# VectorE and ScalarE take the two halves of a step in turn, and TensorE puts the down matmuls between them

## The chip, the cores and the metric

The kernel runs on one core of a Trainium2 chip. The metric is the device time of one launch in microseconds (us). Before the change three runs took 914.65, 913.26 and 915.80 us, median 914.65.

## The reference, cut to what matters

The program is a small hybrid network on x of shape (4, 512, 128), float32. It has four layers, each with a layernorm before it and a residual after it: a state-space layer, a mixture of experts (MoE), an attention layer with 16 heads, and the same mixture of experts once more. The change touches only the two MoE layers, which compute

```
logits = xt @ router_w.T                 # xt: 2048 tokens x 128
topk_vals, topk_idx = top_k(logits, 2)
g = sigmoid(topk_vals); g = g / (g.sum(-1, keepdims=True) + 1e-10)
for e in range(8):
    ge = sum(where(topk_idx == e, g, 0), -1)
    h = silu(xt @ w_gate[e]) * (xt @ w_up[e])      # 256 wide
    out = out + ge[:, None] * (h @ w_down[e])
```

## The kernel before, in words

Every expert is computed for all tokens and weighted with its gate, which is zero where the token did not choose it. Work is laid out by channel: a step s is one expert (s // 4) and one block of 512 tokens (s % 4), so a MoE layer has 32 steps. The hidden width of 256 is two halves m = 0, 1 of 128 rows. Both matmul operands are split into a high part, rounded to fp32r, and the rest, so each product is three matmuls of 128x512.

A step runs through five queues. Each queue issues in the order in which it is written, and semaphores tie them together:

- TensorE, `moe_tensor`: `gate_up` writes, for each half, a gate bank and an up bank (L222 to L224, 12 matmuls), then `down` does the 6 matmuls (L410) of step s - 2 into the token block's own bank, which adds up over the experts. `gate_up` of half m waits for the product of half m of the step before, since that empties the banks; at an expert's first block it also waits for `w`, the split weights of the expert.
- ScalarE, `moe_scalar`: silu of each gate bank (L464), then the rounding of both halves of the gated hidden values to `hid_hi` (L471).
- VectorE, `moe_vector`: `products`, silu times up bank (L521), for both halves; then `gated`, times the expert's gate values (L527), for both halves. The gate values stand in `gate_all`, one copy for each parity of the expert, filled by a broadcast DMA.
- GpSimd, `moe_pool`: `hid_lo = hid - hid_hi` (L654), for both halves. Ahead of these two, at three blocks of four, it splits one of three pieces (256 columns) of the next expert's weights into `w_hi` (L629, times one) and `w_lo` (L632, the rest). The third piece raises `w`.
- SyncE, `moe_sync`: loads the raw weights and the gate values of the expert after next.

Steps 0 to 3 are written out by hand, interleaved with routing and with the layernorm of the last token block; steps 4 to 7 and 24 to 31 are unrolled, those between run in a loop. After step 31 the sums of the four token blocks are copied by ScalarE (`sums`, L475), transposed by TensorE (`sums_turn`, L417) and added to x by VectorE (L566). In the first MoE layer the layernorm of block 0 follows at once, and attention starts from it.

Of the kernel before, what the change touches and what calls it, by code (L numbers as in the profile page):

```python
# [15 lines left out]
ACT = mybir.ActivationFunctionType  # L16
ALU = mybir.AluOpType

P = 128
BANK = 512  # L20
# [13 lines left out]
def build(nc, t, out):  # L34
# [17 lines left out]
    with ExitStack() as ctx:  # L52
# [328 lines left out]
        def moe_tensor(pe, k, meanwhile):  # L381


            q, ln = MOE[k], 2 * k + 1

            def gate_up(i, j, first):
# [4 lines left out]
                for m in range(MT):  # L391
# [36 lines left out]
            gate_up(0, 1, True)  # L428
            ln_turn(pe, ln, 3)
            gate_up(0, 2, True)  # L430
            route_logits(pe, k, 3)
            route_turn(pe, k, 3)
            down(0, 2, True)
            down(0, 3, True)
            route_gates(pe, k, 3)
            gate_up(0, 3, True)
            for j in range(4, 8):
                gate_up(0, j, True)
                down(0, j, True)
            with pe.Fori(1, HALF - 1) as i:  # L440
                for j in range(8):
                    gate_up(i, j, False)
                    down(i, j, False)
            for j in range(8):
                gate_up(HALF - 1, j, False)
                down(HALF - 1, j, False)

            sums_turn(0)
            down(HALF, 0, False)
            sums_turn(1)  # L450
            down(HALF, 1, False)
            sums_turn(2)
            sums_turn(3)

        def moe_scalar(act, k):

            q, ln = MOE[k], 2 * k + 1

            def silus(s, first):
                for m in range(MT):  # L460
                    act.wait_ge(q["g"], 2 * s + m + 1)
                    if not first:
                        act.wait_ge(q["mul"], 2 * s - 1 + m)
                    nc.scalar.activation(silu[:, m, :], bank[2 * m][:, :], ACT.Silu).then_inc(q["sg"], 1)  # L464

            def highs(s, buf, first):
                for m in range(MT):
                    act.wait_ge(q["gm"], 2 * s + m + 1)
                    if not first:
                        act.wait_ge(q["d"], s - 1)  # L470
                    nc.scalar.copy(hid_hi[:, buf, m, :], hid[:, buf, m, :]).then_inc(q["hi"], 1)  # L471

            def sums(c):
                act.wait_ge(q["d"], (E - 1) * CH + c + 1)
# [16 lines left out]
            gates_copy(act, k, 3)  # L491
            highs(2, 0, False)
            silus(3, False)
            highs(3, 1, False)
            for j in range(4, 8):
                silus(j, False)
                highs(j, j % 2, False)
            with act.Fori(1, HALF - 1) as i:
                for j in range(8):
                    silus(8 * i + j, False)  # L500
                    highs(8 * i + j, j % 2, False)
            for j in range(8):
                s = 8 * (HALF - 1) + j
                silus(s, False)
                if j == 7:
                    sums(0)
                highs(s, j % 2, False)
            for c in range(1, CH):
                sums(c)

        def moe_vector(dve, k, last_rows):

            q, ln = MOE[k], 2 * k + 1

            def products(s, buf, first):
                for m in range(MT):
                    dve.wait_ge(q["sg"], 2 * s + m + 1)
                    dve.wait_ge(q["u"], 2 * s + m + 1)
                    if not first:
                        dve.wait_ge(q["hl"], 2 * s - 3 + m)  # L520
                    nc.vector.tensor_tensor(hid[:, buf, m, :], silu[:, m, :], bank[2 * m + 1][:, :],  # L521
                                            ALU.mult).then_inc(q["mul"], 1)

            def gated(s, buf, par, c):
                for m in range(MT):
                    dve.wait_ge(q["mul"], 2 * s + m + 1)
                    nc.vector.tensor_tensor(hid[:, buf, m, :], hid[:, buf, m, :],  # L527
                                            gate_all[:, par, c * BANK:(c + 1) * BANK], ALU.mult).then_inc(q["gm"], 1)
# [27 lines left out]
            first_gates(3)  # L556
            gated(3, 1, 0, 3)
            for j in range(4, 8):
                products(j, j % 2, False)
                gated(j, j % 2, j // CH, j % CH)  # L560
            with dve.Fori(1, HALF) as i:
                body(i)
            for c in range(CH):
# [55 lines left out]
        def moe_pool(pool, k):  # L619
# [1 line left out]

            PIECES = [(0, FH), (FH, 2 * FH), (2 * FH, EW)]

            def split(e_count, ld_value, par, piece, waits):

                lo, hi = PIECES[piece]
                waits()
                pool.wait_ge(q["ld0"] if par == 0 else q["ld1"], ld_value)
# [8 lines left out]
            def body(i, first, last):  # L637
                for j in range(8):
                    s, par, c, buf = 8 * i + j, j // CH, j % CH, j % 2
                    if c < 3 and not (last and par == 1):  # L640

                        def waits():
                            if first and par == 0:
                                return
                            if c < 2:
                                pool.wait_ge(q["u"], 8 * (2 * i + par))
                            else:
                                pool.wait_ge(q["d"], 4 * (2 * i + par))
                        split(2 * i + par + 1, 48 * i + 48 * (1 + par), 1 - par, c, waits)
                    for m in range(MT):  # L650
# [3 lines left out]
                        nc.gpsimd.tensor_tensor(hid_lo[:, buf, m, :], hid[:, buf, m, :],  # L654
                                                hid_hi[:, buf, m, :].bitcast(F32), ALU.subtract).then_inc(q["hl"], 1)

            for piece in range(3):
                split(0, 48, 0, piece, lambda: None)
# [709 lines left out]
```

## Time and profile before

| what | value |
|---|---|
| time of the profiled execution | 913.67 us |
| its span, first to last instruction | 911.9 us |
| median of the three runs | 914.65 us |
| mean granted TensorE clock | 0.966 of full speed |
| TensorE busy, whole span | 823.7 us, 90% |
| VectorE | 646.0 us, 71% |
| ScalarE | 497.5 us, 55% |
| GpSimd | 449.7 us, 49% |
| first MoE layer | about 76 to 243 us of the span |
| second MoE layer | about 745 to 911.9 us |

The busy figures are over the whole span, attention included. What the change is worth is read from the two MoE stretches alone: which engine or wait sets the length of a step there. A TensorE matmul that follows another shows about 0.39 us each but starts 0.23 us after it, so start-to-start times are the ones to use. A group "x2" gives the time of two instructions together.

### The profile page before, as it was taken

The numbers are of one execution on the slowest core, as the hardware profiler recorded it, in microseconds if no ns is written. First come the engines' busy times: TensorE is split into PE (matmuls) and PEld (weight loads), VectorE is DVE, ScalarE is ACT, GpSimd is POOL, SyncE is SP. The second block draws the span as 40 slices with busy tenths as digits, with TensorE's granted clock in tenths as the row PEclk, the third lists the DMA queues.
The fourth block names the chain that finished last, engine by engine and source line by source line (L and its number), as shares of the span: only waits on it lengthen the run. The fifth ranks groups of instructions, "written<-read, shape, count | busy, mean of one in ns | idle before, by whom it ended". The sixth has DMA issues, their size and how long they took to land.

```text
span 911.9 us, 13922 instructions
## 1 busy us (share of the span) xinstructions
PE 823.7 (90%) x4320; PEld 544.0 (60%) x4320; DVE 646.0 (71%) x1664; ACT 497.5 (55%) x1079; POOL 449.7 (49%) x506
## 2 busy tenths in 40 slices
PE   1867689999889999999999999999999995899997
PEld 0555477777655556556556565565555554677776
DVE  7998477767788776767876767767777655667775
ACT  2214354455467766666666665666656634454554
POOL 2350489988334333333333333334333324799984
PEclk9688899999999999999999999999999998999999
DMA  7000335546400000000000000000000012546321
GB/s 208 3 1 28 86 73 81 86 79 205 165 1 1 1 2 1 1 1 1 1 1 1 1 2 1 1 1 1 1 1 1 2 42 72 98 77 79 79 66 46
DMA packets 53265, 36.40 MB, mean 40 GB/s; under 512 B 2209, under 2 KB 50721, under 8 KB 53201
## 3 DMA queue, kind: packets, MB, share of 16 engines
q1 hardware_dynamic: 53200, 35.61, 17.1%
q8 instruction: 33, 0.54, 0.2%
q14 instruction: 32, 0.25, 0.1%
HBM read 34.35 MB, written 1.25 MB: 39 GB/s over the span
## 4 chain that ended last, share of the span: by engine, by line
PE 58%; DVE 13%; issue 12%; POOL 10%; DMA 3%; ACT 2%; POOLq 1%; SPq 0%; ACTq 0%; DVEq 0%
PE bank L805 13%; PE bank L788 11%; PE bank L775 11%; POOL hid_lo L654 7%; PE bank L222 6%; PE bank L224 4%; PE bank L223 4%; PE bank L741 3%; POOL w_hi L629 3%; PE bank L410 2%; DMA gates<-gatesT 1%; DVE x_norm L263 1%; DVE hid L527 1%; DVE hid L521 1%; DMA gate_all<-gates 1%
## 5 line engine op out<-in xcount | busy, mean ns | idle before, releaser
L994 POOL TENSOR_SCALAR prob<-prob,inv_total 128x512 f32<-128x512 f32 x256 | 174.3, 694 | 316.7 <-DVE inv_total L839 316.7
L943 ACT ACTIVATE prob<-prob,peak 128x512 f32<-128x512 f32 x256 | 185.9, 726 | 46.9 <-DVE peak L850 46.9
L654 POOL TENSOR_TENSOR hid_lo<-hid,hid_hi 128x512 fp32r<-128x512 f32 x128 | 163.1, 1294 | 90.5 <-ACT hid_hi L471 90.2
L850 DVE CUSTOM_DVE_ANT_0 prob<-bank,bias_band 128x512 f32<-128x512 f32 x256 | 166.6, 688 | 31.3 <-PE bank L775 25.2
L471 ACT CAST hid_hi<-hid 128x512 fp32r<-128x512 f32 x128 | 78.8, 621 | 140.7 <-DVE hid L527 138.5
L521 DVE TENSOR_TENSOR hid<-silu,bank 128x512 f32<-128x512 f32 x128 | 82.8, 684 | 81.8 <-ACT silu L464 73.8
L805 PE MATMUL bank<-probT,v 128*64 128x512 f32 x512 | 139.2, 624 | 0.8 <-ACT oT L954 0.8
L788 PE MATMUL bank<-ident,prob 128*128 128x128 f32 x1024 | 135.5, 276 | 3.0 <-ACT probT L949 1.8
L788 PEld LDWEIGHTS bank<-ident,prob 128*128 128x128 f32 x1024 | 118.6, 141 | 23.5 <-issue 6.7
L527 DVE TENSOR_TENSOR hid<-hid,gate_all 128x512 f32<-128x512 f32 x128 | 115.9, 944 | 15.8 <-DMA gate_all<-gates 15.8
L222 PE MATMUL bank<-xT_hi,w_hi 128*128 128x512 f32 x256 | 106.8, 417 | 14.1 <-DVE hid L521 14.1
L224 PE MATMUL bank<-xT_hi,w_lo 128*128 128x512 f32 x256 | 103.1, 403 | 0.0
L223 PE MATMUL bank<-xT_lo,w_hi 128*128 128x512 f32 x256 | 102.8, 402 | 0.0
L857 DVE COPY probT<-bank 128x512 f32<-128x512 f32 x128 | 87.6, 684 | 20.7 <-PE bank L788 20.7
L775 PEld LDWEIGHTS bank<-qkT_hi 64*128 64x128 f32 x256 | 24.0, 184 | 101.7 <-issue 93.4
L938 ACT CAST qkT_hi<-bank 128x512 fp32r<-128x512 f32 x64 | 37.7, 589 | 80.0 <-PE bank L224 79.9
L949 ACT COPY probT<-bank 128x512 f32<-128x512 f32 x128 | 73.4, 574 | 14.4 <-PE bank L788 14.4
L464 ACT ACTIVATE silu<-bank 128x512 f32<-128x512 f32 x128 | 69.9, 592 | 6.6 <-PE bank L224 6.3
L222 PEld LDWEIGHTS bank<-xT_hi,w_hi 128*128 128x128 f32 x256 | 49.0, 191 | 38.7 <-DVE hid L521 22.7
L839 DVE RECIPROCAL inv_total<-total 128x2 f32<-128x2 f32 x128 | 21.2, 166 | 65.9 <-ACT prob L943 65.1
L775 PE MATMUL bank<-qkT_hi 64*128 64x512 f32 x256 | 64.4, 500 | 0.0
L224 PEld LDWEIGHTS bank<-xT_hi,w_lo 128*128 128x128 f32 x256 | 49.3, 192 | 11.6
(170 smaller groups left out, 1284.3 us busy)
## 6 DMA issues: line engine op xcount, KB each, us to landing
gate_all<-gates SPq DMA_DIRECT2D x12, 1024.0 KB, 15.6
bias_band<-bias_rows SPq DMA_DIRECT2D x16, 448.0 KB, 11.5
gate_all<-gates SPq DMA_DIRECT2D x16, 256.0 KB, 4.9
w_raw<-in_w_gate SPq DMA_DIRECT2D x16, 128.0 KB, 14.4
w_raw<-in_w_up SPq DMA_DIRECT2D x16, 128.0 KB, 10.7
w_raw<-in_w_down SPq DMA_DIRECT2D x16, 128.0 KB, 8.6
x_res<-in_x SPq DMA_DIRECT2D x4, 256.0 KB, 4.9
out<-x_res SPq DMA_DIRECT2D x4, 256.0 KB, 2.3
```

The costliest lines, as they stand in the source:

```text
L222: nc.tensor.matmul(dst, lh, rh, start=start, stop=False)
L223: nc.tensor.matmul(dst, lh, rl, start=False, stop=False)
L224: return nc.tensor.matmul(dst, ll, rh, start=False, stop=stop)
L521: nc.vector.tensor_tensor(hid[:, buf, m, :], silu[:, m, :], bank[2 * m + 1][:, :], ALU.mult).then_inc(q["mul"], 1)
L527: nc.vector.tensor_tensor(hid[:, buf, m, :], hid[:, buf, m, :], gate_all[:, par, c * BANK:(c + 1) * BANK], ALU.mult).then_inc(q["gm"], 1)
L654: nc.gpsimd.tensor_tensor(hid_lo[:, buf, m, :], hid[:, buf, m, :], hid_hi[:, buf, m, :].bitcast(F32), ALU.subtract).then_inc(q["hl"], 1)
L775: last = nc.tensor.matmul(bank[2 * (n % 2) + h][:, :], ql[rows, u % 2, 0, q], kl[rows, u % 2, 1, :], start=(i == 0), stop=(i == 2))
L788: last = nc.tensor.transpose(bank[4 + h][:, j * P:(j + 1) * P], prob[:, n % PROBS, h, j * P:(j + 1) * P], ident[:, :])
L805: last = nc.tensor.matmul(bank[PV_BANK][h * DK:(h + 1) * DK, :], v[:, kt, col], probT[:, u % 2, h, kt, :], start=(kt == 0), stop=(kt == QT ...
L850: nc.vector.tensor_tensor_reduce(out=prob[:, buf, h, :], in0=bank[2 * (n % 2) + h][:, :], in1=row_bias, scale=-1.0, scalar=NEG_START, op0= ...
L943: nc.scalar.activation(prob[:, buf, h, :], prob[:, buf, h, :], ACT.Exp, bias=peak[:, buf, h:h + 1], scale=-1.0, accum_out=total[:, buf, h: ...
L994: nc.gpsimd.tensor_scalar(prob[:, buf, h, :], prob[:, buf, h, :], inv[:, buf, h:h + 1], 1.0, ALU.mult, ALU.mult).then_inc(a_n, 1)
```

## The change

Four things are done to the same computation.

1. TensorE: a step is now gate and up of half 0, then `down` of step s - 2, then gate and up of half 1 (steps 4 to 31).
2. VectorE: product of half 0, gating of half 0, product of half 1, gating of half 1 (steps 4 to 31). At an expert's first block the wait for the gate values moves ahead of the first product.
3. ScalarE: silu of half 0, rounding of half 1 of the step before, silu of half 1, rounding of half 0. After step 31 the copy of the first sum stands ahead of the last rounding.
4. GpSimd: the split of a weight piece moves from ahead of both subtractions to between them, while its waits stay ahead of the first. `w_hi` is made by a tensor_scalar (times the per-partition one, times 1.0) where it was a tensor_tensor with the one broadcast.

```diff
+            def step(i, j, first):
+                gate_up(i, j, first, [0])
+                down(i, j, first)
+                gate_up(i, j, first, [1])
...
             with pe.Fori(1, HALF - 1) as i:
                 for j in range(8):
-                    gate_up(i, j, False)
-                    down(i, j, False)
+                    step(i, j, False)
...
+            def step(s, j):
+                silu_of(s, 0, False)
+                high(s - 1, (j - 1) % 2, 1, False)
+                silu_of(s, 1, False)
+                high(s, j % 2, 0, False)
...
-                silus(s, False)
-                if j == 7:
-                    sums(0)
-                highs(s, j % 2, False)
+                step(8 * (HALF - 1) + j, j)
+            sums(0)
+            high(8 * HALF - 1, 1, 1, False)
...
+            def step(s, j):
+                for m in range(MT):
+                    product(s, j % 2, m, False)
+                    gate(s, j % 2, m, j // CH, j % CH)
...
                 for j in range(8):
-                    products(8 * i + j, j % 2, False)
                     if j % CH == 0:
                         dve.wait_ge(q["bc0"] if j < CH else q["bc1"], 16 * i)
-                    gated(8 * i + j, j % 2, j // CH, j % CH)
+                    step(8 * i + j, j)
...
-                nc.gpsimd.tensor_tensor(w_hi[:, par, lo:hi], w_raw[:, par, lo:hi], ones[:, :].to_broadcast([P, hi - lo]),
+                nc.gpsimd.tensor_scalar(w_hi[:, par, lo:hi], w_raw[:, par, lo:hi], ones[:, :], 1.0, ALU.mult,
                                         ALU.mult).then_inc(q["sp"], 1)
...
+                    splits = c < 3 and not (last and par == 1)
+                    for m in range(MT):
+                        if m == 0 and splits:
+
+                            pool.wait_ge(q["ld1"] if par == 0 else q["ld0"], 48 * i + 48 * (1 + par))
...
                         nc.gpsimd.tensor_tensor(hid_lo[:, buf, m, :], hid[:, buf, m, :],
                                                 hid_hi[:, buf, m, :].bitcast(F32), ALU.subtract).then_inc(q["hl"], 1)
-
+                        if m == 0 and splits:
+                            split(2 * i + par + 1, 1 - par, c)
```

## Rows read from the trace of the kernel before

**Rows 1.** Windows view, one expert: window, length, busy time of PE, PEld, DVE, ACT, POOL.
```profile
163.00:181.00 18.00, 17.52 (x74) 13.34 (x73) 12.90 (x18) 8.91 (x17) 16.48 (x15) 1.00 0.46 85
```

**Rows 2.** Waits, 120 to 232 us: us in total, times, longest.
```profile
ACT hid_hi L471 <- DVE hid L527: 55.1, 42, 2.5
```

**Rows 3.** Chain that ended last, 140 to 180 us: start us, us, what.
```profile
158.33 1.11 DVE hid L527
...
159.99 0.60 ACT silu L464
...
160.70 0.70 DVE hid L521
...
161.44 0.50 PE bank L222
```

**Rows 4.** Timeline of PE in step 15, starts of steps 16 and 20: start us, us.
```profile
161.78 0.39 PE L223 MATMUL bank<-xT_lo,w_hi 128*128 128x512 f32 x1
162.01 0.39 PE L224 MATMUL bank<-xT_hi,w_lo 128*128 128x512 f32 x1
...
166.12 0.50 PE L222 MATMUL bank<-xT_hi,w_hi 128*128 128x512 f32 x1 [0.25 <-DVE hid L521]
...
183.99 0.50 PE L222 MATMUL bank<-xT_hi,w_hi 128*128 128x512 f32 x1 [0.24 <-DVE hid L521]
```

**Rows 5.** Timeline of DVE, gatings beside a weight split and a shorter pair.
```profile
161.90 2.20 DVE L527 TENSOR_TENSOR hid<-hid,gate_all 128x512 f32<-128x512 f32 x2
...
170.84 1.78 DVE L527 TENSOR_TENSOR hid<-hid,gate_all 128x512 f32<-128x512 f32 x2
```

**Rows 6.** Timeline of POOL, the same stretch.
```profile
159.99 2.54 POOL L654 TENSOR_TENSOR hid_lo<-hid,hid_hi 128x512 fp32r<-128x512 f32 x2
162.50 1.06 POOL L629 TENSOR_TENSOR w_hi<-w_raw,ones 128x256 fp32r<-128x256 f32 x1
163.63 1.07 POOL L632 TENSOR_TENSOR w_lo<-w_raw,w_hi 128x256 fp32r<-128x256 f32 x1
```

**Rows 7.** Timeline, ACT and then POOL: a rounding and the subtraction it releases.
```profile
225.22 1.22 ACT L471 CAST hid_hi<-hid 128x512 fp32r<-128x512 f32 x2 [1.63 <-DVE hid L527]
225.91 2.55 POOL L654 TENSOR_TENSOR hid_lo<-hid,hid_hi 128x512 fp32r<-128x512 f32 x2 [1.28 <-ACT hid_hi L471]
```

**Rows 8.** Groups by shape on POOL: count, busy us, mean ns.
```profile
L994 POOL TENSOR_SCALAR prob<-prob,inv_total 128x512 f32<-128x512 f32 x256 | 174.3, 694 | 316.7 <-DVE inv_total L839 316.7
...
L1168 POOL TENSOR_TENSOR bT_hi<-bT,ones 128x256 fp32r<-128x256 f32 x1 | 0.6, 612 | 0.1
...
L1168 POOL TENSOR_TENSOR router_hi<-ssm_par,ones 128x8 fp32r<-128x8 f32 x1 | 0.2, 197 | 0.0
```

**Rows 9.** Timeline: gatings of step 3 (DVE), start of step 5 (PE).
```profile
113.44 1.29 DVE L527 TENSOR_TENSOR hid<-hid,gate_all 128x512 f32<-128x512 f32 x2 [4.25 <-DMA gate_all<-gates]
116.66 0.50 PE L222 MATMUL bank<-xT_hi,w_hi 128*128 128x512 f32 x1 [3.50 <-DVE hid L521]
```

**Rows 10.** Timeline of step 31, first MoE: PE, PE, ACT, DVE, DVE.
```profile
232.42 0.40 PE L222 MATMUL bank<-xT_hi,w_hi 128*128 128x512 f32 x1
...
240.16 0.50 PE L410 MATMUL bank<-hid_hi,w_hi 128*128 128x512 f32 x1 [0.85 <-POOL hid_lo L654]
...
234.00 1.32 ACT L464 ACTIVATE silu<-bank 128x512 f32<-128x512 f32 x2
...
235.57 0.69 DVE L521 TENSOR_TENSOR hid<-silu,bank 128x512 f32<-128x512 f32 x1 [0.17 <-PE bank L224]
...
237.38 0.69 DVE L566 TENSOR_TENSOR x_res<-bank,x_res 128x512 f32<-128x512 f32 x1
```

**Rows 11.** Timeline of PE, starts of steps 5 and 31, second MoE.
```profile
782.06 0.50 PE L222 MATMUL bank<-xT_hi,w_hi 128*128 128x512 f32 x1 [3.10 <-DVE hid L521]
...
897.67 0.40 PE L222 MATMUL bank<-xT_hi,w_hi 128*128 128x512 f32 x1
```

**Rows 12.** DMA issues: count, KB each, median us to landing.
```profile
gate_all<-gates SPq DMA_DIRECT2D x12, 1024.0 KB, 15.6
```

More of the change, by code:

```diff
@@ L384, in moe_tensor, with gate_up @@
             q, ln = MOE[k], 2 * k + 1
-            def gate_up(i, j, first):
+            def gate_up(i, j, first, halves=range(MT)):
                 s, par, c = 8 * i + j, j // CH, j % CH
@@ L390, in gate_up @@
                     pe.wait_ge(q["w"], 2 * i + par + 1)
-                for m in range(MT):
+                for m in halves:
                     if not (first and j == 0):
@@ L436, in moe_tensor @@
             gate_up(0, 3, True)
+            def step(i, j, first):
+                gate_up(i, j, first, [0])
+                down(i, j, first)
+                gate_up(i, j, first, [1])
             for j in range(4, 8):
-                gate_up(0, j, True)
-                down(0, j, True)
+                step(0, j, True)
             with pe.Fori(1, HALF - 1) as i:
                 for j in range(8):
-                    gate_up(i, j, False)
-                    down(i, j, False)
+                    step(i, j, False)
             for j in range(8):
-                gate_up(HALF - 1, j, False)
-                down(HALF - 1, j, False)
+                step(HALF - 1, j, False)
             sums_turn(0)
@@ L457, in moe_scalar, with silu_of, high @@
             q, ln = MOE[k], 2 * k + 1
+            def silu_of(s, m, first):
+                act.wait_ge(q["g"], 2 * s + m + 1)
+                if not first:
+                    act.wait_ge(q["mul"], 2 * s - 1 + m)
+                nc.scalar.activation(silu[:, m, :], bank[2 * m][:, :], ACT.Silu).then_inc(q["sg"], 1)
             def silus(s, first):
                 for m in range(MT):
[L461 to L464, printed above, removed]
+                    silu_of(s, m, first)
+            def high(s, buf, m, first):
+                act.wait_ge(q["gm"], 2 * s + m + 1)
+                if not first:
+                    act.wait_ge(q["d"], s - 1)
+                nc.scalar.copy(hid_hi[:, buf, m, :], hid[:, buf, m, :]).then_inc(q["hi"], 1)
             def highs(s, buf, first):
                 for m in range(MT):
[L468 to L471, printed above, removed]
+                    high(s, buf, m, first)
+            def step(s, j):
[3 more added lines that the diff above has]
+                high(s, j % 2, 0, False)
             def sums(c):
@@ L513, in moe_vector, with product, gate @@
             q, ln = MOE[k], 2 * k + 1
+            def product(s, buf, m, first):
+                dve.wait_ge(q["sg"], 2 * s + m + 1)
+                dve.wait_ge(q["u"], 2 * s + m + 1)
+                if not first:
+                    dve.wait_ge(q["hl"], 2 * s - 3 + m)
+                nc.vector.tensor_tensor(hid[:, buf, m, :], silu[:, m, :], bank[2 * m + 1][:, :],
+                                        ALU.mult).then_inc(q["mul"], 1)
             def products(s, buf, first):
                 for m in range(MT):
[L517 to L522, printed above, removed]
+                    product(s, buf, m, first)
+            def gate(s, buf, m, par, c):
+                dve.wait_ge(q["mul"], 2 * s + m + 1)
+                nc.vector.tensor_tensor(hid[:, buf, m, :], hid[:, buf, m, :],
+                                        gate_all[:, par, c * BANK:(c + 1) * BANK], ALU.mult).then_inc(q["gm"], 1)
             def gated(s, buf, par, c):
                 for m in range(MT):
-                    dve.wait_ge(q["mul"], 2 * s + m + 1)
-                    nc.vector.tensor_tensor(hid[:, buf, m, :], hid[:, buf, m, :],
-                                            gate_all[:, par, c * BANK:(c + 1) * BANK], ALU.mult).then_inc(q["gm"], 1)
+                    gate(s, buf, m, par, c)
+            def step(s, j):
+                for m in range(MT):
+                    product(s, j % 2, m, False)
+                    gate(s, j % 2, m, j // CH, j % CH)
             def body(i):
                 for j in range(8):
-                    products(8 * i + j, j % 2, False)
                     if j % CH == 0:
                         dve.wait_ge(q["bc0"] if j < CH else q["bc1"], 16 * i)
-                    gated(8 * i + j, j % 2, j // CH, j % CH)
+                    step(8 * i + j, j)
             def first_gates(c):
@@ L558, in moe_vector @@
             for j in range(4, 8):
-                products(j, j % 2, False)
-                gated(j, j % 2, j // CH, j % CH)
+                step(j, j)
             with dve.Fori(1, HALF) as i:
@@ L622, in moe_pool, with split @@
             PIECES = [(0, FH), (FH, 2 * FH), (2 * FH, EW)]
-            def split(e_count, ld_value, par, piece, waits):
+            def split(e_count, par, piece):
                 lo, hi = PIECES[piece]
-                waits()
-                pool.wait_ge(q["ld0"] if par == 0 else q["ld1"], ld_value)
-                nc.gpsimd.tensor_tensor(w_hi[:, par, lo:hi], w_raw[:, par, lo:hi], ones[:, :].to_broadcast([P, hi - lo]),
+                nc.gpsimd.tensor_scalar(w_hi[:, par, lo:hi], w_raw[:, par, lo:hi], ones[:, :], 1.0, ALU.mult,
                                         ALU.mult).then_inc(q["sp"], 1)
@@ L639, in body @@
                     s, par, c, buf = 8 * i + j, j // CH, j % CH, j % 2
[L640 to L645, printed above, removed]
+                    splits = c < 3 and not (last and par == 1)
+                    for m in range(MT):
+                        if m == 0 and splits:
+                            pool.wait_ge(q["ld1"] if par == 0 else q["ld0"], 48 * i + 48 * (1 + par))
+                            if not (first and par == 0) and c < 2:
                                 pool.wait_ge(q["u"], 8 * (2 * i + par))
-                            else:
+                            elif not (first and par == 0):
                                 pool.wait_ge(q["d"], 4 * (2 * i + par))
-                        split(2 * i + par + 1, 48 * i + 48 * (1 + par), 1 - par, c, waits)
-                    for m in range(MT):
                         pool.wait_ge(q["hi"], 2 * s + m + 1)
@@ L655, in body @@
                                                 hid_hi[:, buf, m, :].bitcast(F32), ALU.subtract).then_inc(q["hl"], 1)
+                        if m == 0 and splits:
+                            split(2 * i + par + 1, 1 - par, c)
+            pool.wait_ge(q["ld0"], 48)
             for piece in range(3):
-                split(0, 48, 0, piece, lambda: None)
+                split(0, 0, piece)
             body(0, True, False)
```

8 lines of the change are left out of this document (2 added, 6 removed).

## The prediction

> **What bounds the kernel now.** I read the page first for where the change lies: two MoE layers, about 167 us each. The windows view of one expert [rows 1] shows TensorE busy 17.5 of 18 us, GpSimd 16.5, VectorE only 12.9. That looks like a full TensorE, but start to start a matmul takes 0.23 us [rows 4], so the 18 matmuls of a step need 18 x 0.232 = 4.18 us, and step 15 to step 16 takes 4.68 [rows 3, 4]. Four steps take 17.87 us (166.12 to 183.99, steps 16 to 20 [rows 4]) against 16.7 of matmul issue.
>
> What fills the 0.5 us is in the waits and the chain. ScalarE waits for VectorE's gating 42 times, 55 us in all [rows 2], and TensorE at each of these starts for VectorE's product [rows 4]. The chain [rows 3] gives the loop: second gating ends 159.44, rounding, silu 159.99 (0.53 after the rounding began), product 160.70 (0.71 later), next step's first matmul 161.44 (0.74 later). VectorE then does two products (160.70 to 161.90, 1.20) and two gatings (2.20) [rows 5]. Sum: 0.02 + 0.53 + 0.71 + 1.20 + 2.20 = 4.66. So in the old order silu(s+1, 0) stands behind both roundings of step s, and all of VectorE's step is in that loop.
>
> The 2.20 hides a second limit. Gatings take 1.10 us each there, but two took 1.78 where no split went before, and 0.60 each, start to start, where GpSimd is idle (235.57 plus 0.60, two gatings, 237.38 [rows 10]). Put the rows of VectorE and GpSimd side by side [rows 5, 6]: subtractions 159.99 to 162.50; gating asked for at 161.90 moves at 162.50 and is through at 163.03; w_hi, started 162.50, ends at 163.56 though such a split takes 0.61 alone [rows 8]; the next gating ends at 164.1; w_lo at about 164.67; then the next subtraction. The two engines go strictly in turn. Holding times are 1.25 for a subtraction, 0.53 for a gating, 0.53 for w_hi, 0.57 for w_lo, and 2 x 1.25 + 2 x 0.53 + 0.53 + 0.57 + 0.02 = 4.68, which is the step. Products, which read a PSUM bank, are always 0.69 and take no part.
>
> This is where the Trainium skill speaks against the change. "SBUF — State Buffer", section "Who interferes with whom", says that GpSimd and a VectorE instruction with two SBUF inputs share one port pair as an exclusive lock, held for the whole instruction. The trace agrees: 1.06 and 1.07 for splits that take 0.61 and 0.72 alone. By a reading without that rule (gating always 0.6) the new order would leave nothing but matmul issue.
>
> **The change, part by part.** I take the loops of the new order with these times. Let gate and up of half 0 of an expert's first step start at 0.
>
> *TensorE.* Same instructions. Half 0 from 0 (0.11 longer after a stall, 0.34 against 0.23 [rows 3, 4]), down 1.5, half 1 2.9, next step 4.29. Product(s, 0) has until then, so the old wait of TensorE for products goes: product comes at about 1.9 and 4.7.
>
> *ScalarE.* silu starts 0.45 after the third matmul of its bank starts: in step 31 that matmul starts at 232.42 + 8 x 0.232 = 234.28 and the second silu at 235.32 - 0.59 = 234.73 [rows 10]. So silu(s, 1) starts at 2.89 + 0.46 + 0.45 = 3.8, and rounding(s, 0) stands behind it, at 4.3, though its gating was through at about 3.3. Subtraction(s, 0) follows 0.69 after the rounding [rows 7], at 5.0. This cost is new: TensorE now brings half 1 1.39 us later, and half 0 waits with it.
>
> *VectorE.* Same instructions. A gating now directly follows its own product, so the product's whole 0.69 plus about 0.04 counts and not 0.60: estimate 0.13 more for each half. VectorE has room: 2 x (0.73 + 0.53) plus port waits, in 4.18. I put it at nothing by itself; it is in the walk below.
>
> *GpSimd.* The tensor_scalar of 256 columns is not in the trace. 512 columns take 694 ns, and a tensor_tensor with the broadcast one takes 197 at 8 columns and 612 at 256 [rows 8]. Below: half of 694, 347 ns, with 0.08 less holding as for the old w_hi, or 0.27. Above: no saving, 0.53. On a line from 197 at 8 to 694 at 512 it is 197 + 497 x 248/504 = 442 ns; with 0.05 off, between the two offsets seen (0.08 for w_hi, 0.04 for the subtraction), I take holding 0.39. That is nearest to the row of its own kind. The Trainium skill ("GPSIMD Engine Reference", section 3.1) gives about 1.03 cycles per element at 1.2 GHz for one input. Its slope taken from the 694 would give 0.47 us alone, so 0.42 held, and 1 us more in the sum.
>
> *The weight split is moved behind subtraction(s, 0).* This is the step that decides. TensorE's first step of the next expert waits for the third piece (w_lo of block 2). Everything from subtraction of block 0 to there goes through the port, in turn with the gatings that ask meanwhile. Walk: subtraction(0, 0) 5.00 to 6.25; gating(0, 1), asked 5.37, to 6.78; w_hi to 7.17, 0.07 own wait, w_lo to 7.81; gating(1, 0) to 8.34; subtraction(0, 1) to 9.59; gating(1, 1) to 10.12; subtraction(1, 0) to 11.37; gating(2, 0) to 11.90; split to 12.93; subtraction(1, 1) to 14.18; gating(2, 1) to 14.71; subtraction(2, 0) to 15.96; gating(3, 0) to 16.49; split to 17.52. As a sum: 5.00 + 5 x 1.25 + 6 x 0.53 + 3 x (0.39 + 0.07 + 0.57) = 17.52. TensorE would be there at 16.70. In the old order the split ended at 164.67 and step 16 started at 166.12, 1.45 us to spare. So the new order trades 17.87 for 17.57 per expert: TensorE runs three steps at 4.18 to 4.29 and then stalls about 0.87 for `w`.
>
> *From step 5 to step 31.* Before: 232.42 - 116.66 = 115.76 and 897.67 - 782.06 = 115.61 [rows 9 to 11], which is 26 x 4.18 = 108.7, 1.67 of step 5 (it takes 5.85 in both layers, partly at the lower clock after TensorE's wait; unchanged) and 5.3 of stalls. The old kernel had little loss in its first and last steps; the new one stalls at each of six expert boundaries (steps 8, 12, ... 28). After: 108.7 + 1.67 + 6 x 0.87 = 115.6. Difference -0.1 per layer, where a full cure would be -5.3.
>
> *Step 5.* Gatings of step 3 end their wait for the DMA at 113.44 [rows 9], and silu(4, 0) stood behind two roundings; now behind one: -0.53 per layer.
>
> *End of a layer.* Half 1 of step 31 comes after down of step 29. Let step 31 start at 0. silu(31, 1) 3.7, product(31, 1) 4.5 (0.59 after the last up matmul starts [rows 10]), gating asked 5.26; subtraction(31, 0) asks at 5.23 and, if first, holds until 6.48. Then the gating is through at 7.0, and only then comes VectorE's first add to x, which was at 237.38 - 232.42 = 4.96. The last down starts at 9.05 (before: 240.16 - 232.42 = 7.74). If the gating is first, they are 6.15 and 8.35. The requests are 0.03 apart, so I take the middle. The layernorm of block 0 hangs on the add, and attention on it: +1.6 in the first layer. In the second the last down decides: +0.95.
>
> *DMAs.* None changes, but VectorE now waits for an expert's gate values before its first product. They are asked for when the expert before last is gated: from 6.0 of one step to 1.9 of the fifth step after, 5 x 4.36 + 1.9 - 6.0 = 17.7 us, against 15.6 to landing [rows 12]. Hidden, with 2 us to spare.
>
> *Sum.* 2 x (-0.1 - 0.53) + 1.6 + 0.95 = +1.3. On the profiled execution 913.67 that is 915.0; it lies 1.0 under the median of the runs, so I forecast 914.65 + 1.3 = 916.
>
> **Rivals.** (A) The forecast: the `w` wait takes the place of the loop over VectorE and ScalarE. Bounds of the split's holding, 0.27 to 0.53, change the three splits of six experts in two layers, 36 x 0.12 = -4.3 to 36 x 0.14 = +5.0; the middle of that and the tail's 0.8 either way give 912 to 920.
> (B) TensorE becomes the bound: the split is in time because gatings find the port free (fewer than six in the chain; two fewer are enough with a cheaper w_hi). For it: 16.5 of 18 us of GpSimd shrinks by 3 x 0.14 per expert, and the old split had 1.45 us to spare. Against: the walk. Full price 2 x (-5.3 - 0.53) + 2.55 = -9.1, so 905.5; half cured 910.
> (C) Slower: the tensor_scalar is no cheaper in the chain than the broadcast (holding 0.53). Its place is the chain from subtraction(0, 0) to `w`; price 36 x 0.14 = +5.0 and the tail's upper end +0.8: 922. Slower by over 0.3% from a holding of 0.39 + 1.4/36 = 0.43 on. For it: hardly anything under 0.43 is proved by a row; against: 694 ns at 512 columns.
> (D) The gate values' wait, now ahead of the product: if landing exceeds 17.7 us by one, six loads in two layers cost 12 us, 928. The median of 15.6 speaks against.
> That the change does not do what it says, the two engines staying in lockstep through the port, would give A's time too.
>
> **How the numbers follow.** A measurement of this kernel can tell about 0.3%, 2.7 us: below 911.9 and above 917.4. A 0.55 (within 0.38, slower 0.10, faster 0.07), B 0.25 (faster), C 0.17 and D 0.03 (slower). Faster 0.32, same 0.38, slower 0.30. The range 906 to 922 leaves out the fullest form of B and the far ends of C and D; A alone is 912 to 920.
>
> **What would show it.** Right: steps of 4.18 three times and one of about 4.9 at each expert's start, TensorE's idle time there put down to GpSimd's w_lo (L632 in the old file), no more waits of TensorE for products; subtraction(s, 0) starting about 5.0 after its step; w_hi about 0.44 where alone. Wrong: boundary steps of 4.18 (B), a w_hi of 0.6 (C), VectorE waiting for gate_all inside the loop (D), or a gating that overlaps a subtraction, which would break the walk's rule of turns.

## The result, and the profile after

The changed kernel takes 919.37 us (median of 18 runs, 916.22 to 922.79) against 914.75 for the kernel before: ratio 1.0049, 95% interval 1.0037 to 1.0061, so 4.6 us slower. The forecast was 916.0, 1.3 us more than before and within what counts as no change. The time lies in the forecast's range; the loss is three and a half times the one forecast, and the interval leaves no doubt that it is a loss.

The profiled execution took 920.07 us, span 918.2 (before 913.67 and 911.9). The first thing to look at is where TensorE's steps start. Timeline of PE in the changed kernel, starts of steps 16 to 20, which answer to [rows 4]:

```profile
168.05 0.49 PE L222 MATMUL bank<-xT_hi,w_hi 128*128 128x512 f32 x1 [0.44 <-POOL w_lo L649]
...
172.32 0.40 PE L222 MATMUL bank<-xT_hi,w_hi 128*128 128x512 f32 x1
...
176.49 0.39 PE L222 MATMUL bank<-xT_hi,w_hi 128*128 128x512 f32 x1
...
180.74 0.39 PE L222 MATMUL bank<-xT_hi,w_hi 128*128 128x512 f32 x1
...
182.54 0.50 PE L410 MATMUL bank<-hid_hi,w_hi 128*128 128x512 f32 x1 [0.24 <-POOL hid_lo L669]
...
186.03 0.50 PE L222 MATMUL bank<-xT_hi,w_hi 128*128 128x512 f32 x1 [0.43 <-POOL w_lo L649]
```

The steps take 4.27, 4.17, 4.25 and 5.29: three at TensorE's own pace, and one long one that ends in a wait for `w_lo`, the last piece of the next expert's weights. The long step loses time twice: `down` (the line at 182.54) starts 0.41 us late because it waits for `hid_lo` of two steps before, then the next step starts 0.60 late for `w_lo`, and a restart after a wait costs 0.11. The forecast had the whole loss as one wait for `w`. Both hang on the same queue of GpSimd and `w_lo` comes last, so the end of that queue still sets the length. An expert takes 17.98 us, where it took 17.87. The old pattern, a stall for VectorE's product at two steps of four [rows 4], is gone.

The waits of the same stretch, 120 to 235 us, answer to [rows 2]: who waited for whom, us in total, times, longest.

```profile
ACT silu L465 <- PE bank L224: 39.5, 49, 2.6
DVE hid L530 <- PE bank L224: 16.1, 19, 2.3
ACT hid_hi L475 <- DVE hid L539: 15.1, 22, 1.2
DVE hid L530 <- POOL hid_lo L669: 7.4, 6, 1.3
POOL hid_lo L669 <- ACT hid_hi L475: 5.8, 9, 1.3
PEld bank L410 <- POOL hid_lo L669: 4.8, 11, 0.7
PEld bank L222 <- issue: 3.5, 4, 0.9
PE bank L222 <- POOL w_lo L649: 2.5, 6, 0.5
PEld bank L222 <- POOL w_lo L649: 1.6, 2, 0.8
PE bank L410 <- POOL hid_lo L669: 1.2, 5, 0.2
```

ScalarE waited 55 us for gatings before and 15 now; silu and product now wait mostly for TensorE. TensorE has two new waits, both for GpSimd: the matmul that waits for `w_lo`, six times, once at each expert boundary, and `down` that waits for `hid_lo` (4.8 us of its weight loads and 1.2 of its matmuls; waits of loads overlap matmuls, so these do not add up). The change does what it says, and the wait that ends last at a boundary is the forecast's.

The chain that leads to it, GpSimd's timeline (answers to [rows 6]):

```profile
173.08 1.29 POOL L669 TENSOR_TENSOR hid_lo<-hid,hid_hi 128x512 fp32r<-128x512 f32 x1 [0.52 <-ACT hid_hi L475]
174.34 0.92 POOL L646 TENSOR_SCALAR w_hi<-w_raw,ones 128x256 fp32r<-128x256 f32 x1
175.35 0.74 POOL L649 TENSOR_TENSOR w_lo<-w_raw,w_hi 128x256 fp32r<-128x256 f32 x1
176.05 3.45 POOL L669 TENSOR_TENSOR hid_lo<-hid,hid_hi 128x512 fp32r<-128x512 f32 x2
179.48 0.92 POOL L646 TENSOR_SCALAR w_hi<-w_raw,ones 128x256 fp32r<-128x256 f32 x1
180.49 0.74 POOL L649 TENSOR_TENSOR w_lo<-w_raw,w_hi 128x256 fp32r<-128x256 f32 x1
181.19 2.99 POOL L669 TENSOR_TENSOR hid_lo<-hid,hid_hi 128x512 fp32r<-128x512 f32 x2
184.16 0.92 POOL L646 TENSOR_SCALAR w_hi<-w_raw,ones 128x256 fp32r<-128x256 f32 x1
185.17 0.73 POOL L649 TENSOR_TENSOR w_lo<-w_raw,w_hi 128x256 fp32r<-128x256 f32 x1
```

Read it against the walk of the prediction. The first subtraction of the expert starts 173.08 - 168.05 = 5.03 us after its step (5.00 forecast). From it on the chain holds five subtractions (the four behind the first are two pairs, 3.45 and 2.99 instead of 2.5 because gatings go between), three w_hi of 0.92 and three w_lo, and TensorE starts 0.13 after the last w_lo ends at 185.90. GpSimd has no idle time in between but 0.09 between each w_hi and its w_lo. The windows view of this expert, columns as in [rows 1], has GpSimd, its waits for the port included, at 17.2 of 18.0 us, more than TensorE's matmul issue of 16.7:

```profile
168.05:186.03 17.98, 17.31 (x72) 13.32 (x73) 13.94 (x17) 9.41 (x17) 17.21 (x15) 1.00 0.34 84
```

At the end of the first layer (answers to [rows 10]): step 31 starts at 234.47, and the lines are of PE, DVE, DVE.

```profile
234.47 0.39 PE L222 MATMUL bank<-xT_hi,w_hi 128*128 128x512 f32 x1
...
243.52 0.50 PE L410 MATMUL bank<-hid_hi,w_hi 128*128 128x512 f32 x1 [0.21 <-POOL hid_lo L669]
...
239.74 1.73 DVE L539 TENSOR_TENSOR hid<-hid,gate_all 128x512 f32<-128x512 f32 x1
241.38 0.68 DVE L585 TENSOR_TENSOR x_res<-bank,x_res 128x512 f32<-128x512 f32 x1
```

The last gating took 1.73 where it takes 0.69 alone: the subtraction was first at the port. The first add to x comes 6.91 us after step 31 starts (before 4.96), the last down 9.05 (before 7.74).

### The profile page after: what moved, and what is told of

It reads as the page before. It is cut to its first block, busy times and chain, and to the rows that moved or that the text cites. A ratio compares the mean times of both kernels' runs of the same rounds, so it can differ in the third digit from the quotient of the medians.

```text
span 918.2 us, 13922 instructions
## 1 busy us (share of the span) xinstructions
PE 826.7 (90%) x4320; PEld 545.8 (59%) x4320; DVE 667.8 (73%) x1664; ACT 503.2 (55%) x1079; POOL 462.9 (50%) x506
## 4 chain that ended last, share of the span: by engine, by line
PE 57%; POOL 16%; DVE 11%; issue 10%; DMA 3%; ACT 2%; POOLq 1%; SPq 0%; ACTq 0%; DVEq 0%
PE bank L823 13%; PE bank L806 11%; PE bank L793 11%; POOL hid_lo L669 11%; PE bank L222 6%; PE bank L224 4%; PE bank L223 4%; POOL w_hi L646 4%; PE bank L759 3%; PE bank L410 3%; DMA gates<-gatesT 1%; POOL w_lo L649 1%; DVE x_norm L263 1%; DMA gate_all<-gates 1%; DVE ln_stats L237 1%
## 5 line engine op out<-in xcount | busy, mean ns | idle before, releaser
L669 POOL TENSOR_TENSOR hid_lo<-hid,hid_hi 128x512 fp32r<-128x512 f32 x128 | 193.8, 1532 | 81.8 <-ACT hid_hi L475 81.8
L539 DVE TENSOR_TENSOR hid<-hid,gate_all 128x512 f32<-128x512 f32 x128 | 133.7, 1050 | 20.2 <-DMA gate_all<-gates 16.3
L530 DVE TENSOR_TENSOR hid<-silu,bank 128x512 f32<-128x512 f32 x128 | 86.9, 684 | 60.4 <-PE bank L224 32.7
L465 ACT ACTIVATE silu<-bank 128x512 f32<-128x512 f32 x128 | 76.0, 598 | 87.0 <-PE bank L224 86.9
L222 PE MATMUL bank<-xT_hi,w_hi 128*128 128x512 f32 x256 | 104.8, 409 | 13.4 <-DVE hid L530 8.4
L410 PE MATMUL bank<-hid_hi,w_hi 128*128 128x512 f32 x128 | 55.4, 433 | 3.6 <-POOL hid_lo L669 3.5
```

Of the source, the lines that this page charges most:

```text
L222: nc.tensor.matmul(dst, lh, rh, start=start, stop=False)
```

## The experiments

All kernels were timed in five rounds beside the kernel before; a ratio is to that kernel, with its 95% interval. Its median was 914.95 us beside experiments 1, 2, 3 and 5, 914.23 beside 6, 7, 8 and 10, and 915.22 beside 4, 9 and 11. Lengths of steps and experts are of one profiled execution each.

**1. The changed kernel with the old w_hi.**

```diff
-                nc.gpsimd.tensor_scalar(w_hi[:, par, lo:hi], w_raw[:, par, lo:hi], ones[:, :], 1.0, ALU.mult,
-                                        ALU.mult).then_inc(q["sp"], 1)
+                nc.gpsimd.tensor_tensor(w_hi[:, par, lo:hi], w_raw[:, par, lo:hi], ones[:, :].to_broadcast([P, hi - lo]),
+                                        ALU.mult).then_inc(q["sp"], 1)
```

> The changed kernel with w_hi made by the old tensor_tensor (times the broadcast one); all else as changed. My theory: TensorE's stall at an expert's first step is the end of a chain of subtractions, gatings and splits that take GpSimd's and VectorE's port in turn, and each w_hi in it holds 0.53 instead of 0.39 us. So three splits per expert add 0.42 us to the 17.98 of an expert, 6 boundaries in two layers 5 us: about 9.5 us over the kernel before (+1.0%), boundary steps of 5.7 us. Rival 1, the stall is made by TensorE's and ScalarE's new order alone and GpSimd only follows: no difference from the changed kernel, +4.6 us. Rival 2, the tensor_scalar itself is what costs: back to the kernel before or under it.

Measured: 923.24 us, ratio 1.0094 (1.0068 to 1.0119), 8.3 us over before. w_hi takes 1.06 again, an expert 18.35 us (starts of steps 16 and 20 at 165.59 and 183.94). Three w_hi, each 0.14 us longer, make an expert 0.37 longer, so nearly all of it goes into TensorE's wait. So the chain through the port is what TensorE waits for, and rivals 1 and 2 fall.

**2. The changed kernel with the split ahead of the first subtraction.**

```diff
-                        if m == 0 and splits:
-                            split(2 * i + par + 1, 1 - par, c)
+                    if splits:
+                        split(2 * i2 + par + 1, 1 - par, c)
```

Here i2, par and c are those of the next step; the waits of the split stand ahead of the second subtraction, and the first split of a layer is done at once.

> The changed kernel with each split piece put back ahead of its step's first subtraction (right behind the last subtraction of the step before, its waits ahead of that subtraction), tensor_scalar kept. My theory: the chain to the third piece loses one subtraction and one gating (1.72 us), and GpSimd does w_hi in the 0.5 to 1.3 us in which it waited for the first rounding. TensorE's `w` stall goes, and the port's total sets the pace, about 17.45 us per expert against 17.98: 2 to 3 us under the kernel before, 7 under the changed one. Rival 1 (the order of the other engines alone): stays at +4.6. Rival 3 (the two engines' total port time is the limit wherever the split stands): 17.9 per expert, 1 us from the changed kernel.

Measured: 911.41 us, ratio 0.9965 (0.9949 to 0.9982): 3.5 us under before, about 8 under the changed kernel. An expert takes 17.34 us (164.71 to 182.05). GpSimd's timeline of it:

```profile
169.84 0.47 POOL L646 TENSOR_SCALAR w_hi<-w_raw,ones 128x256 fp32r<-128x256 f32 x1
170.40 0.74 POOL L649 TENSOR_TENSOR w_lo<-w_raw,w_hi 128x256 fp32r<-128x256 f32 x1
171.10 3.46 POOL L670 TENSOR_TENSOR hid_lo<-hid,hid_hi 128x512 fp32r<-128x512 f32 x2
174.54 0.48 POOL L646 TENSOR_SCALAR w_hi<-w_raw,ones 128x256 fp32r<-128x256 f32 x1
175.10 1.06 POOL L649 TENSOR_TENSOR w_lo<-w_raw,w_hi 128x256 fp32r<-128x256 f32 x1
...
179.10 0.92 POOL L646 TENSOR_SCALAR w_hi<-w_raw,ones 128x256 fp32r<-128x256 f32 x1
180.10 0.74 POOL L649 TENSOR_TENSOR w_lo<-w_raw,w_hi 128x256 fp32r<-128x256 f32 x1
```

Two of the three w_hi now meet no gating (0.47 and 0.48 us instead of 0.92), and one subtraction fewer stands in the chain to the third piece. Of the parts undone in these experiments the new place of the split cost most. The remaining stall (4.70 at the first step of each expert) is for hid_lo; the wait for `w_lo` is gone. The expectation held, with a little more gain than expected; rivals 1 and 3 fall. The new orders of VectorE and of ScalarE were never undone alone, so what each is worth is open.

**3. The kernel before with only the tensor_scalar.** The split's waits stand one subtraction earlier, as in experiment 2.

> The kernel before with only w_hi changed to a tensor_scalar (the split stands where it stood, its waits one subtraction earlier). My theory: each of three splits per expert gives 0.14 us back to the port, so steps of 4.66 become 4.5: 36 x 0.13 = 4.6 us under the kernel before, 910. Rival 2 (the tensor_scalar costs): slower than before. Rival 4 (the old loop over VectorE and ScalarE, 4.66, does not hang on the port): no difference.

Measured: 917.75 us, ratio 1.0034 (1.0019 to 1.0049), slower. This expectation failed. Timelines of DVE and POOL in that kernel:

```profile
162.62 2.26 DVE L527 TENSOR_TENSOR hid<-hid,gate_all 128x512 f32<-128x512 f32 x2
...
163.72 1.44 POOL L627 TENSOR_SCALAR w_hi<-w_raw,ones 128x256 fp32r<-128x256 f32 x1
165.24 0.74 POOL L630 TENSOR_TENSOR w_lo<-w_raw,w_hi 128x256 fp32r<-128x256 f32 x1
```

Both gatings went ahead of the tensor_scalar, which ended at 165.16, 0.28 after the second one. With the tensor_tensor [rows 5, 6] one gating went ahead of w_hi and one ahead of w_lo, and w_lo's own start-up lay behind the latter. Now w_lo starts into a free port and pays it: 2.53 + 1.44 + 0.08 + 0.69 = 4.74 a step against 4.68. So the turns are not strict, though my prediction had them so. Why the tensor_scalar lets both pass was not tried.

**4. The control to 3: same placement, w_hi by the old tensor_tensor.**

> The control to the run of the kernel before with tensor_scalar, which was slower by 2.8 us where 4.6 us of gain were expected: the same placement (split behind the last subtraction of the step before, its waits one subtraction earlier), but w_hi by the old tensor_tensor. My reading now: in that run the tensor_scalar took 1.44 us beside two gatings, both of which went ahead of it, so its short holding was given back by w_lo starting cold. Then this control is equal to the kernel before within 0.2%. Rival: the moved waits cost, then this one is slower by 2 to 3 us too.

Measured: 915.84 us, ratio 1.0011 (0.9998 to 1.0023). DVE and POOL in this kernel, at the same place as in 3:

```profile
162.32 2.20 DVE L527 TENSOR_TENSOR hid<-hid,gate_all 128x512 f32<-128x512 f32 x2
...
162.90 1.08 POOL L627 TENSOR_TENSOR w_hi<-w_raw,ones 128x256 fp32r<-128x256 f32 x1
164.06 1.07 POOL L630 TENSOR_TENSOR w_lo<-w_raw,w_hi 128x256 fp32r<-128x256 f32 x1
```

The moved waits explain at most a small part. The intervals of 3 and 4 touch, so the times alone don't settle the rest; the profiles do: steps 16 to 20 take 18.05 us in 3, 17.83 here and 17.87 before, and both w_hi and w_lo have their old lengths here. With the placement the same, the longer steps are the tensor_scalar's.

**5. `w` raised after the second piece.**

```diff
-                if piece == 2:
+                if piece == 1:
                     last.then_inc(q["w"], 1)
+                if piece == 2:
+                    last.then_inc(q["wd"], 1)
```

> The changed kernel with `w` raised after the second piece (gate and up weights), and a semaphore of its own for the third, on which the down matmuls and the next load wait. My theory: the wait of TensorE at an expert's first step goes, but GpSimd is busy 17.2 of 18 us per expert with its waits for the port, so the subtractions become late instead and TensorE waits for hid_lo: 17.8 per expert, +2 us on the kernel before, 2 to 3 us under the changed one. Rival 5 (the `w` wait is the whole loss): 16.7 per expert, 7 us under the kernel before. Rival 1 (order alone): +4.6.

Measured: 916.28 us, ratio 1.0014 (0.9999 to 1.0029), 17.80 us per expert (163.45 to 181.25), as expected. The longest wait of TensorE in it, in total:

```profile
PEld bank L412 <- POOL hid_lo L673: 8.1, 15, 0.7
```

The `w` wait is gone, and the wait of down for hid_lo, 4.8 us in the changed kernel, grew to 8.1: it now comes at two steps of an expert, the first and the last, 0.4 us each. An expert is only 0.18 us shorter. The semaphore was only where GpSimd's queue showed.

**6. ScalarE makes w_hi, in the new order.**

```diff
+            def weights_high(i, j, last):
...
+                nc.scalar.copy(w_hi[:, 1 - par, lo:hi], w_raw[:, 1 - par, lo:hi]).then_inc(q["sp"], 1)
...
                 high(s, j % 2, 0, False)
+                weights_high(i, j, last)
```

> The changed kernel, but from step 4 on ScalarE makes w_hi (a copy, after its rounding of half 0), and GpSimd only w_lo. My theory (the port's turns set the pace): each split leaves 0.9 us less on GpSimd and one turn of the port less, GpSimd's work falls under TensorE's, the `w` wait goes and an expert takes TensorE's own 16.7 us. Together 9 to 10 us under the kernel before, 905; what stays is the longer end of a layer (1.2 us in the first). Rival 1 (the order of the queues alone costs): no better than +4.6. Rival 6 (ScalarE becomes late, 9.4 of 18 us busy plus 3 x 0.37): TensorE waits for silu or product, 17.5 or more per expert.

**7. The same in the old order**, `weights_high` between silus and highs.

> The kernel before, but from step 4 on ScalarE makes w_hi between its silus and its roundings, and GpSimd only w_lo; queues otherwise in the old order. My theory: the old loop over VectorE and ScalarE (two products, two gatings, rounding, silu: 4.66) shrinks to 3.7 to 4.2 once gatings wait less for the port, so TensorE's 4.18 bounds: 10 us under the kernel before, 904, equal to the same edit in the new order or 0.6 better by its shorter end. Rival 7 (the old order is bound by its own loop whatever the port does, so the new order is needed for the gain): 4.5 per step, at most 4 us under before, and clearly over the same edit in the new order.

Measured: 905.10 us, ratio 0.9891 (0.9871 to 0.9912), and 904.80 us, ratio 0.9894 (0.9874 to 0.9913). Windows of one expert in each, new order first:

```profile
161.23:177.97 16.74, 16.74 (x73) 13.37 (x72) 12.91 (x16) 10.31 (x21) 15.38 (x12) 1.00 0.50 79
```

```profile
163.86:180.58 16.72, 16.72 (x74) 13.56 (x72) 11.62 (x17) 9.75 (x19) 13.54 (x12) 1.00 0.57 87
```

TensorE is busy all the time in both, at 4.18 a step. w_hi costs ScalarE 0.41 us, and GpSimd is at 13.5 to 15.4 us. Both orders reach the same 16.7, so the order of the queues is not what kept the kernel before from it. In the old order the pairs of gatings take 1.3 to 1.9 us instead of up to 2.2, and the loop over VectorE and ScalarE is shorter by as much. Rivals 1, 6 and 7 fall.

**8. The kernel before with only TensorE's new order.**

```diff
-                    gate_up(i, j, False)
+                    gate_up(i, j, False, [0])
                     down(i, j, False)
+                    gate_up(i, j, False, [1])
```

> The kernel before with only TensorE's queue in the new order (gate and up of half 0, down, half 1). My theory: half 1 comes 1.39 us later, its silu and product too, and both gatings and all GpSimd work of the step stand behind it; port turns and the loop then give about 18.3 us per expert: 7 to 9 us over the kernel before. Rival 2 (order on TensorE is free, the loss is in the moved split): no difference from the kernel before.

Measured: 926.84 us, ratio 1.0116 (1.0093 to 1.0140), 12.6 us slower, where 7 to 9 were expected. Steps 16 to 20 start 18.18 us apart (167.75 to 185.93), and the five experts of steps 8 to 28 take 18.28 on average, as expected. In the profiled execution the two layers' ends are 1.4 us longer each, which the expectation left out, and attention, which the edit doesn't touch, took 503.1 us against 498.8; why stays open. One turn of the loop, DVE, DVE, ACT, PE:

```profile
172.38 0.69 DVE L524 TENSOR_TENSOR hid<-silu,bank 128x512 f32<-128x512 f32 x1 [0.80 <-POOL hid_lo L657]
172.98 1.88 DVE L530 TENSOR_TENSOR hid<-hid,gate_all 128x512 f32<-128x512 f32 x2
...
174.36 1.15 ACT L474 CAST hid_hi<-hid 128x512 fp32r<-128x512 f32 x2 [2.24 <-DVE hid L530]
...
176.88 0.50 PE L222 MATMUL bank<-xT_hi,w_hi 128*128 128x512 f32 x1 [0.52 <-DVE hid L524]
```

The product of half 1 comes late, both gatings stand behind it, both roundings behind them, and the next step's silu and product behind those. A rounding that waits 2.24 us is no sign by itself: before, the longest waited 2.5 [rows 2]. What is longer is TensorE's own wait for the product, here 0.68 us late by its start, against 0.36 to 0.52 in the kernel before.

**9. The changed kernel with TensorE's old order.**

> The changed kernel with TensorE's queue back in the old order (gate and up of both halves, then down); VectorE, ScalarE and GpSimd as changed. My theory: half 1 comes 1.39 us earlier, so its silu, the rounding of half 0 behind it and the whole port chain start earlier; the `w` stall shrinks to about 0.4 us more than TensorE's own time per expert of 17.2 to 17.6 us: within 1 us of the kernel before, 4 us under the changed one. Rival (TensorE's order is what lets products come in time): slower than the changed kernel.

Measured: 916.34 us, ratio 1.0012 (0.9995 to 1.0029), 17.69 us per expert (167.17 to 184.86). The time is as expected; the expert is just above the expected 17.2 to 17.6, and the way is another than I named:

```profile
ACT hid_hi L474 <- PE bank L410: 39.2, 25, 2.4
```

The rounding of half 0 waits for down of step s - 2, which frees hid_hi and comes last in TensorE's old order. So the first subtraction starts 5.31 us after its expert's first step (172.48 - 167.17), not earlier than 5.03. What is shorter is the chain behind it, 12.38 us against 12.95, with five gatings in it instead of six. TensorE then waits only for `w_lo`. TensorE's new order costs the changed kernel about 3 us (0.3%), though it takes away the wait of the rounding for down.

**10. Short splits.** The changed kernel, splits of experts 2 to 7 cut to 8 of 256 columns.

> The changed kernel with the weight splits of experts 2 to 7 cut to the first 8 of each piece's 256 columns (the rest of the split is left out, so stale weights are used); all waits, queues and semaphores stay. It measures what the splits' port time costs. My theory: with about 0.4 us per split instead of 1.7, TensorE bounds at 4.18 a step: 8 to 9 us under the kernel before. Rival 1 (the order costs by itself, splits or not): +4.6, or at least slower than before.

Measured: 904.11 us, ratio 0.9885 (0.9863 to 0.9906), 16.7 us per expert from step 8 on, 4.18 a step. Between the first and the last steps of a layer the order costs nothing once the splits' port time is gone.

**11. The end of a layer in the old order**, in the changed kernel and in that of experiment 6: TensorE gate_up of both halves before down, VectorE products before gatings, the first sum ahead of both roundings, in step 31 only.

> The changed kernel with only the last step of each layer back in the old order. My theory: of the change's loss the two ends make 1.95 and 1.3 us; they go, the `w` stalls stay: about 1.5 us over the kernel before (+0.15%), 3 us under the changed one. Rival: the ends are hidden, then no difference from the changed kernel.

> The changed kernel with w_hi made by ScalarE from step 4 on (as in the earlier run of that edit in the new order, 905.1), and its last step of each layer in the old order: TensorE gate and up of both halves, then down; VectorE both products, both gatings; ScalarE the first sum ahead of both roundings. My theory: the end of a layer grew because the last gating waits behind a subtraction for the port; with it back (first add to x at 5.0 instead of 6.8 us after step 31 starts, last down at 7.8 instead of 9.0) 2 to 3 us come off: about 903, the fastest of all. Rival: the end of the first layer is hidden by other work, then 904.5.

Measured: 919.59 us, ratio 1.0047 (1.0029 to 1.0065), and 904.34 us, ratio 0.9884 (0.9863 to 0.9905). Against the changed kernel (1.0049) and experiment 6 (0.9891) no difference can be told. Timeline of DVE at the end of the first layer of the former, where step 31 starts at 233.06:

```profile
234.04 1.77 DVE L544 TENSOR_TENSOR hid<-hid,gate_all 128x512 f32<-128x512 f32 x1
235.72 0.68 DVE L535 TENSOR_TENSOR hid<-silu,bank 128x512 f32<-128x512 f32 x1
...
238.90 0.68 DVE L593 TENSOR_TENSOR x_res<-bank,x_res 128x512 f32<-128x512 f32 x1
```

The last gating of step 30 still waits for a subtraction (1.77) and step 31 inherits it; the add comes at 5.84 instead of 6.91, not 4.96. In the profiled executions the end gives back 0.5 us of the way to attention's first matmul (14.43 after step 31's start, 14.98 in the changed kernel, 13.56 before) and 0.45 in the second layer. My expectations of 3 us and of 2 to 3 us were wrong.

## Why the prediction was right in kind and off in size

**The bound of the kernel before.** Right, with a correction. Port turns and the VectorE-ScalarE loop give 4.68 at the two steps of four that stall; experiments 6, 7 and 10 take work off the port and reach 4.18. I had called the port a "second limit"; experiment 7 shows it was the only one that had to go: shorter gatings shorten the loop too. The lock is there as the Trainium skill ("SBUF — State Buffer", section "Who interferes with whom") has it: 1.06 us for a w_hi beside a gating and 0.61 alone. Its rule spoke for the right side. My addition that the turns are strict fell in experiment 3.

**The new stall.** Right in place and, but for the wait of down for hid_lo, in kind. Forecast were 5.00 us to the first subtraction, six gatings in the chain, 0.92 for a w_hi behind a gating (0.39 + 0.53) and a boundary step of 4.9; the rows show 5.03, six, 0.92 and 5.3.

**The term that was too small: w_lo at 0.57 us.** That figure came from [rows 6], where w_lo stood behind a gating and its start-up was hidden. In the changed kernel no gating goes between w_hi and w_lo, and w_lo takes 0.70 from its start to the next one, and 0.73 to its end where TensorE waits for it. Three of them are 0.4 us per expert; TensorE's start after it adds 0.08, w_hi's completion 0.06, and the five subtractions give back 0.2. So the chain measures 17.98, not 17.57, and steps 5 to 31 take 234.47 - 116.90 = 117.57 us and 902.72 - 785.67 = 117.05, where 115.6 was forecast and 115.76 and 115.61 were measured before. These are 1.8 and 1.4 us over before, against -0.1 each in the forecast. The five experts from step 8 to step 28 take 17.94 each, where 17.57 was forecast; that is 1.8 us more per layer. From the start of step 5 to that of step 8 it took 15.23 and 14.73, forecast 15.08. That this came so near was luck: step 5 was taken as unchanged at 5.85 us and took 6.12 and 4.76. In the second layer the granted clock was 1.00 there (780 to 792 us); before it was 0.87 (776 to 789), and matmuls from 783.3 to 786.7 start 0.43 us apart, at the lower of the clock's two levels.

**w_hi.** 0.474 us alone (fastest of 48), forecast 0.442. The forecast's 0.39 of holding fits the 0.92, but by two errors that cancel: 0.03 too short alone, and 0.05 taken off where the rows give 0.08. The Trainium skill ("GPSIMD Engine Reference", section 3.1) led to 0.47, and the trace agrees with it.

**Step 5.** Forecast -0.53 per layer. From the start of step 3 to that of step 5 the first layer went from 12.27 to 12.18 us, the second from 11.85 to 11.16. The DMA before it moved as well (gatings of step 3 at 114.28, not 113.44), so the first layer's gain was eaten.

**The end.** The add's delay was forecast at 1.6 as the middle of a race; the race was lost in both layers, as in the forecast's own worse case (last gating through at 7.0, last down at 9.05): 1.95 and 1.31 against 1.6 and 0.95. But only 1.4 of the 1.95 reach attention (its first matmul 14.98 us after step 31 starts, before 13.56). An instruction of the layernorm that ran beside a subtraction before now meets none. Timeline of DVE, before and after:

```profile
239.42 0.71 DVE L248 TENSOR_SCALAR ln_var<-ln_mean_var 128x4 f32<-128x4 f32 x1
```

```profile
243.42 0.17 DVE L248 TENSOR_SCALAR ln_var<-ln_mean_var 128x4 f32<-128x4 f32 x1
```

So the 1.6 was near what counts, by luck. Experiment 11 shows that part of the delay is carried over from step 30 and that undoing it cannot be told in the time.

**The sum.** In the profiled executions: steps 5 to 31 1.8 + 1.4, ends 1.4 + 1.3, start of step 5 -0.1 - 0.7, together 5.1 of 6.4 us, and attention 1.3 more; over 18 runs the loss is 4.6. Attention, which the change does not touch, took 500.2 us from its first matmul to the second MoE layer against 498.8; in the profiled executions of the experiments it took 498.8 to 503.1, in no order that follows the edits. What moves it stays open, and so does which part of the 4.6 it holds. The cause is shown for the steps of the MoE layers, not for this part.

**Rivals.** B (TensorE bound) did not come: all six gatings are in the chain. C's price per w_hi holds: experiment 1 is 3.7 us over the changed kernel, where C's 36 x 0.14 gives 5.0, within its interval. D did not come: no wait for gate_all is in the loop's list. My chances gave slower by over 0.3% only 0.30; what was slower was the forecast's own mechanism with a term too small, which its range "up to 920" held.

## What to carry to other kernels

Before reordering queues, add up the time that two engines spend on a resource they share, instruction by instruction; if the sum is near the step, an order only moves the wait, and taking one instruction off the resource (here 0.41 us of ScalarE) gives all that the reordering aimed at, in either order. When work that another engine waits for once in a while is moved behind something, walk the whole chain to it, not its own delay alone. A duration read where an instruction waits hides its start-up; take the figure from a place where it runs alone as well.

## What the runs showed of the hardware

- A GpSimd tensor_scalar of 128x256 takes 0.47 us alone, a tensor_tensor with a broadcast operand 0.61; beside one waiting gating they take 0.92 and 1.06.
- The turns of GpSimd and VectorE are not strict: two gatings back to back both passed ahead of a started tensor_scalar (1.44 us), while only one passed ahead of a tensor_tensor (1.06 us). A cheaper instruction made the kernel slower: by 0.34% against the kernel before, and 0.23% against the control (experiments 3 and 4).
- ScalarE's copies (128x256, 36 of them, 0.40 to 0.41 us) ran beside both engines without lengthening: w_hi moved there costs neither of them a turn. In experiment 7 the pair of subtractions that runs beside the copy at 175.40 takes 2.55 us (from 174.00), as ever.
